# One arithmetic step instead of two in GpSimd's score shift, and an exponential without a scale

## The reference, cut to what matters

```python
scores = jnp.einsum('bqhd,bkhd->bhqk', q, k) * scale
decay = jnp.exp(-alpha * lag * DT)
scores = scores * decay
attn = jax.nn.softmax(scores, axis=-1)      # exp(scores - max(scores)) / sum
out = jnp.einsum('bhqk,bkhd->bqhd', attn, v)
```

## Time and profile before

| | |
|---|---|
| median of 3 runs | 241.84 us |
| the profiled execution | 241.85 us |
| its span, first to last instruction | 240.1 us |
| mean granted TensorE clock | 0.997 of full speed |
| TensorE matmul busy | 226.1 us (94%) |
| VectorE busy | 190.9 us (80%) |
| GpSimd busy | 190.2 us (79%) |
| ScalarE busy | 163.3 us (68%) |

### The profile page before, as it was taken

One profiled execution on the slowest core, in us unless ns is written; L12 is line 12 of the kernel. 1 busy time (PEld: TensorE's weight loads), 2 busy tenths in 40 slices (PEclk: granted clock), 3 DMA queues, 4 the chain that ended last, 5 costly groups with the idle time before them and its releaser, 6 DMA issues.

```text
span 240.1 us, 5810 instructions
## 1 busy us (share of the span) xinstructions
PE 226.1 (94%) x1830; PEld 167.3 (70%) x1830; DVE 190.9 (80%) x791; ACT 163.3 (68%) x321; POOL 190.2 (79%) x345
## 2 busy tenths in 40 slices
PE   7997999998999998999999899999999999999994
PEld 7775567665567676557677567677888888688882
DVE  3599788896998889999979988468756886976763
ACT  4447867777867799867887678586657658565550
POOL 6489988999999999997999999618486644676661
PEclk9999999999999999999999999999999999999998
DMA  5717814742006632005734450015323340026211
GB/s 140 222 33 175 282 76 96 200 114 79 0 4 141 191 85 72 0 4 127 201 71 139 165 191 3 3 45 147 108 76 125 122 131 3 0 102 197 104 44 44
DMA packets 16302, 24.38 MB, mean 102 GB/s; under 512 B 3280, under 2 KB 5968, under 8 KB 16144
## 3 DMA queue, kind: packets, MB, share of 16 engines
q1 hardware_dynamic: 15840, 24.01, 34.4%
q10 hardware_dynamic: 432, 0.01, 0.1%
HBM read 13.39 MB, written 1.18 MB: 61 GB/s over the span
## 4 chain that ended last, share of the span: by engine, by line
PE 41%; POOL 39%; DVE 12%; ACT 3%; issue 3%; DVEq 0%; ACTq 0%
PE bank L916 41%; POOL sc L298 34%; DVE sc L711 4%; POOL rstd L271 3%; POOL wgu_sb L307 1%; DVE sc L880 1%; DVE attn_t L634 1%; DVE qk L626 1%; DVE qk_st L808 1%; ACT xn L372 1%; POOL nmr L276 1%; DVE mx L711 1%; POOL nmean L269 1%; ACT L575 1%; DVE cw L703 1%
## 5 line engine op out<-in xcount | busy, mean ns | idle before, releaser
L298 POOL TENSOR_SCALAR sc<-sc,mx 128x256 f32<-128x256 f32 x256 | 122.2, 495 | 4.2 <-DVE mx L711 4.1
L711 DVE CUSTOM_DVE_ANT_0 sc<-bank,decay 128x256 f32<-128x256 f32 x256 | 91.0, 418 | 13.6 <-PE bank L916 13.4
L405 ACT ACTIVATE pr<-bank 128x512 f32<-128x512 f32 x128 | 69.4, 595 | 23.2 <-PE bank L916 23.1
L916 PE MATMUL bank<-id_f,sc 128*128 128x128 f32 x512 | 69.9, 278 | 4.0 <-ACT pr L405 1.9
L347 POOL TENSOR_TENSOR act_lo<-sc,act_hi 128x512 fp32r<-128x512 f32 x35 | 45.2, 1296 | 33.0 <-ACT act_hi L566 33.0
L916 PEld LDWEIGHTS bank<-id_f,sc 128*128 128x128 f32 x512 | 55.8, 141 | 18.7 <-issue 8.7
L916 PE MATMUL bank<-pr,v_one 128*32 128x256 f32 x512 | 34.3, 385 | 0.0
L874 DVE TENSOR_TENSOR pr<-bank,cwb 128x512 f32<-128x512 f32 x32 | 22.0, 687 | 14.3 <-PE bank L916 14.0
L575 ACT ACTIVATE bank<-bank 128x512 f32<-128x512 f32 x32 | 18.6, 582 | 19.0 <-PE bank L916 18.7
L880 DVE TENSOR_TENSOR sc<-pr,bank 128x512 f32<-128x512 f32 x36 | 24.7, 687 | 5.8 <-ACT bank L575 2.6
L916 PE MATMUL bank<-h_hi,wgu_hi 128*128 128x512 f32 x72 | 28.5, 395 | 0.0
(11 more groups left out here) (108 smaller groups left out, 274.9 us busy)
## 6 DMA issues: line engine op xcount, KB each, us to landing
cwb<-cw_dram SPq DMA_DIRECT2D x64, 128.0 KB, 3.0
qk_st<-qk SPq DMA_DIRECT2D x60, 128.0 KB, 2.7
wgu_sb<-in_w_gu SPq DMA_DIRECT2D x1, 1152.0 KB, 5.6
wgu_sb<-in_x_t SPq DMA_DIRECT2D x4, 256.0 KB, 3.5
x_all<-in_x SPq DMA_DIRECT2D x1, 768.0 KB, 6.9
o_sum<-o_t SPq DMA_DIRECT2D x6, 128.0 KB, 2.3
o_val<-o_t SPq DMA_DIRECT2D x6, 128.0 KB, 2.2
out_dram<-wgu_sb SPq DMA_DIRECT2D x3, 256.0 KB, 3.3
```

The costliest lines, as they stand in the source:

```text
L298: last = nc.gpsimd.tensor_scalar(sc[:, n % RING, t, :], sc[:, n % RING, t, :], -1.0, mx[:, n % RING, t:t + 1], ALU.mult, ALU.add)
L405: nc.scalar.activation(pr[:, n % RING, :, :].rearrange("p a b -> p (a b)"), turn_bank(i, n)[:], ACT.Exp, scale=-1.0).then_inc(s["exp_done" ...
L711: last = nc.vector.tensor_tensor_reduce(sc[:, n % RING, t, :], ps_s[n % SB][:, t * SEQ:t * SEQ + SEQ], decay[:, t, :], float(HD) ** -0.5, ...
L916: return nc.tensor.matmul(o, l, r, start=start, stop=stop, skip_group_check=not check, is_transpose=transpose or None)
```

## The change

GpSimd computes `sc - mx` in one arithmetic step in place of `sc * -1.0 + mx`. The sign of its result is turned round, so ScalarE's exponential loses its scale of -1. Shapes, order, semaphores and counts of instructions are the same.

```diff
@@ negdiff, GpSimd
                     for t in range(BPC):
-                        last = nc.gpsimd.tensor_scalar(sc[:, n % RING, t, :], sc[:, n % RING, t, :], -1.0,
-                                                       mx[:, n % RING, t:t + 1], ALU.mult, ALU.add)
+                        last = nc.gpsimd.tensor_scalar(sc[:, n % RING, t, :], sc[:, n % RING, t, :],
+                                                       mx[:, n % RING, t:t + 1], None, ALU.subtract)
                     last.then_inc(s["nd_done"], 1)
@@ exps, ScalarE
                     nc.scalar.activation(pr[:, n % RING, :, :].rearrange("p a b -> p (a b)"), turn_bank(i, n)[:],
-                                         ACT.Exp, scale=-1.0).then_inc(s["exp_done"], 1)
+                                         ACT.Exp).then_inc(s["exp_done"], 1)
```

## The result

The changed kernel takes 345.49 us (median of 4 runs, 344.75 to 346.17), the kernel before beside it 241.69 us (median of 4 runs). The ratio is 1.429, 95% interval 1.425 to 1.434. The range on record ended at 284 us.

What follows compares the result with a forecast made beforehand. GpSimd and TensorE together were taken to bound the attention. 256 dearer subtractions add 7.7 us, waits absorb 1.7 and 1.4, so 4.6 us on 241.85 give 246.5 us (chance 0.34); the range was 238 to 284 us.

Steps and rivals of the forecast that it cites:

- The sign: Whole kernel: slower was given a chance of 0.60, faster 0.25, no change 0.15.
- The bound and the waits: Attention: GpSimd and TensorE run side by side; a dearer subtraction is paid almost in full, less GpSimd's 2.7 and 1.4 us waits.
- The exponential: ScalarE's exponential in the attention: dropping its scale costs 0, bounds -1.0 to +1.3 us over 128 instructions.
- columns as dear as now: GpSimd's subtraction: one step adds a fixed 30 ns and leaves the column cost unchanged, 508 ns each, 7.7 us in all.
- The bounds: GpSimd's subtraction at 128 x 256: between 402 ns (-76 each, a fill's slope) and 772 ns (+294, two-tensor difference's slope).
- The slope of the present form: GpSimd's two-step subtraction: each further column costs 1.11 ns, from 478 ns at 256 columns and 198 at 4.
- (D): GpSimd's subtraction: moving columns bounds both forms and overlap hides the fixed difference, so no change, 241.85 us; chance 0.15.
- (C): GpSimd's subtraction: one operation fewer runs nearer a fill's cost, 432 ns, giving 238 us (235 to 241); chance 0.25.
- Rival (B): GpSimd's subtraction: one step is dearer for each column too, 639 ns, giving 279 us, 313 at the upper bound; chance 0.26.
- The reservation: GpSimd's one-step instruction: by spacing from start to start it costs only some 10 ns more, not 30, giving 242.7 us.

Runs made afterwards that it cites:

- kernel of forms by themselves: A kernel that only measures, without the computation: twelve forms of GpSimd's tensor_scalar, six instructions each at three widths; at 256 columns mult-add 484 ns, subtract alone 927.

## Why the prediction was wrong

The sign was right, the size was not: 4.6 us were forecast, 103.8 came (104.2 between the profiled spans).

- **The bound and the waits**: right for a dearer subtraction, which was paid almost in full, less all 4.2 us of GpSimd's waits.
- **The exponential**: right. 597 ns on the median before and after, and the same pace in a kernel of its own.
- **The step that failed** is "columns as dear as now". I read the row of 128 x 4 as a fixed 30 ns and carried the column cost over. At 4 columns the gap is mostly foot (26 to 28 ns, of which 4 x 1.65 = 7 are columns) and says little of the columns: 1.65 ns x 252 = 416 ns of the 443 were not in any row. The term of 256 x 30 ns = 7.7 us measured 110.5 us.
- **The bounds failed too.** The upper one, 772 ns, took its slope of 2.16 ns from the two-tensor difference; the one-step form has 2.49 and 923 ns. I held an instruction that reads less to be no dearer; side by side the difference of two tensors takes 724 ns (L170) and one step on one tensor 927. Only the parenthesis held, that no row excluded a cost of the columns up to 7.5 ns each, and I gave it almost nothing.
- **The slope of the present form** was mis-sized: 1.11 ns from lines 298 and 266, measured 0.83. Line 266 has immediates, line 298 a per-partition scalar, and that is 75 ns on the row at 4 columns (271 against 196) and at 256 (484 against 409). The row of the fill, 0.81, was the one that met it: the pair was already as cheap for a column as a fill or a copy. The argument against (D) and the match that (C) found for its slope both rested on these 1.11 ns.
- **Rival (B)**, dearer for each column, is what happened; its reason, a favoured pair, was right. It was priced at 279 us and 313 at most. With 901 - 458 = 443 ns from start to start it is 256 x 0.443 = 113.4 us, less 4.2: 350.9, and 345.5 came. Of these 5.4 us, 2.0 are at the ends and in line 307. Another 2.9 are single long subtractions, up to 1027 ns: those of before together lay 5.0 us over their pace (122.2 - 256 x 0.458), those of after 2.0 (232.7 - 256 x 0.901). The last 0.5 or so is that the changed kernel's profiled execution, 346.1 us, lay above its median.
- **Rival (C)** has the wrong mechanism, since a body with one operation fewer isn't nearer to a fill but dearer by 443 ns. Its size is wrong as well: with GpSimd freed of 13 us the time fell by 0.8 to 1.4, where I had 4 for 11.8. I had taken TensorE's waits on GpSimd for time that GpSimd owed; with 13.4 us of waiting on GpSimd's side, 7.6 us of them are still there.
- **The reservation** from start to start was sound as method, but it compared starts of unlike instructions. Between six equal ones the pair with immediates and mult alone start 153 and 187 ns apart at 4 columns (L155 and L92, from their rows in order of time): 34 ns, not 10.

## What to carry to other kernels

Don't price GpSimd by the number of arithmetic steps. Its `tensor_scalar` on fp32 costs 0.83 ns a column as mult-add or add-mult, and 2.49, three times as much, with subtract, add or mult alone; at 256 columns mult-mult is with the first (478 ns) and max alone with the second (845). So write a lone add or mult with a neutral partner: mult-add with plus 0.0 has been run here, and with times 1.0. A missing shape can't be priced from one of four columns, nor bounded by another operation's slope: when the form of an instruction changes, take the column cost as unknown and the range wide. And the waits of one full engine on another are not time that the other can give back, until a run with that other made lighter shows it.

## What the runs showed of the hardware that was not expected

- Two steps can be slower than one or twice as fast: at 256 columns add-add takes 1145 ns and mult-mult 478, where subtract alone takes 922.
- An immediate in place of the per-partition scalar takes 75 ns off GpSimd's row. In the kernel the pace doesn't gain by it (476 to 479 against 458 ns); in the kernel of forms by themselves it does (2.3 against 2.8 us for six, L158 and L59). The wait before each step isn't the whole reason: the two subtractions of a step have none between them, and the first two of the kernel with immediates start at 13.20 and 13.67 us, 0.47 apart. What takes the time stays open.
- TensorE, waiting for GpSimd again and again, was granted less of its clock: 0.82 over the attention of the changed kernel and 0.74 in the kernel with mult-subtract, against 1.00 before. In the changed kernel its transposes went from 278 to 324 ns and the products with the values from 385 to 517, and none of that is in the time of the attention, as GpSimd never waited for anything.
